# Scan runs of four fused layers: the last product by C moves to VectorE, and the second half's du is made behind the first units

## What is computed

```python
xdbl = xm @ W_xp
dtr, Bm, Cm = jnp.split(xdbl, [DTR, DTR + DS], axis=-1)
dt = jax.nn.softplus(dtr @ W_dt + b_dt)
A = -jnp.exp(A_log)

def step(hst, inp):
    dt_t, B_t, C_t, x_t = inp
    dA = jnp.exp(dt_t[:, :, None] * A)
    hst = hst * dA + (dt_t * x_t)[:, :, None] * B_t[:, None, :]
    y = jnp.einsum('bds,bs->bd', hst, C_t)
    return (hst, y)
```

## Time and profile before

| | |
|---|---|
| median of 3 runs | 1942.12 us (1942.08 to 1942.58) |
| the profiled execution | 1945.84 us, span of its instructions 1943.5 us |
| busy share of the span | PE 95%, PE weight load 69%, DVE 82%, ACT 73%, POOL 54% |
| mean granted TensorE clock | 0.975 |
| first unit of the scan, last unit (start) | 208.2 us, 1420.5 us |
| runs 0 to 5, first scan | 208.2, 446.3, 669.9, 853.7, 1083.5, 1265.7 us |

### The profile page before, as it was taken

The page is one execution under the profiler, slowest core; times in us unless marked ns, Lnnn a source line. Parts: engine busy times, 40 slices in busy tenths (PEclk is TensorE's granted clock), DMA queues, the critical chain, the costliest instruction groups (busy, mean ns, idle before and its releaser), DMA issues.

```text
span 1943.5 us, 32682 instructions
## 1 busy us (share of the span) xinstructions
PE 1845.3 (95%) x12312; PEld 1337.9 (69%) x12312; DVE 1600.7 (82%) x2125; ACT 1425.8 (73%) x2661; POOL 1048.6 (54%) x603
## 2 busy tenths in 40 slices
PE   6989899999999999999999999999998999999997
PEld 3664899948998599969995799689974333332323
DVE  5565899768998699989995999889987999999742
ACT  3426899468993899799974999799954377777775
POOL 3031599526994299939980699479944400003000
PEclk9989899998999999999999999999999799999999
DMA  5023111021111111101110121021101111111000
GB/s 202 1 85 99 59 57 55 32 72 43 56 59 37 51 54 60 51 24 55 56 44 2 40 60 56 24 72 58 58 15 32 38 42 38 37 37 36 17 23 22
DMA packets 57547, 95.18 MB, mean 49 GB/s; under 512 B 14951, under 2 KB 23559, under 8 KB 55982
## 3 DMA queue, kind: packets, MB, share of 16 engines
q1 hardware_dynamic: 55854, 88.90, 15.2%
q0 software_dynamic: 1536, 4.20, 0.7%
HBM read 73.55 MB, written 6.91 MB: 41 GB/s over the span
## 4 chain that ended last, share of the span: by engine, by line
PE 63%; POOL 14%; ACT 8%; DVE 8%; issue 6%; DMA 1%; SPq 1%; DVEq 0%; ACTq 0%; POOLq 0%
POOL A L1019 13%; PE PS L865 10%; PE PS L840 10%; PE PS L256 8%; PE PS L1603 6%; PE PS L1556 6%; PE PS L1763 5%; PE PS L846 5%; PE PS L265 3%; DVE A L1569 2%; PE PS L441 2%; PE PS L872 1%; ACT A L931 1%; ACT A L908 1%; PE PS L243 1%
## 5 line engine op out<-in xcount | busy, mean ns | idle before, releaser
L1019 POOL TENSOR_TENSOR A<-A 128x1024 f32<-128x1024 f32 x384 | 897.6, 2396 | 223.2 <-ACT small L923 111.0
L931 ACT ACTIVATE A<-A,negA 128x512 f32<-128x512 f32 x768 | 547.3, 715 | 34.0 <-DVE A L1000 24.4
L1000 DVE TENSOR_TENSOR_SCAN A<-A,PS 128x512 f32<-128x512 f32 x384 | 436.2, 1201 | 44.8 <-PE PS L846 23.8
L1000 DVE TENSOR_TENSOR_SCAN A<-A,small,PS 128x512 f32<-128x512 f32 x384 | 451.2, 1259 | 5.3 <-ACT A L931 5.3
L865 PE MATMUL PS<-ident,A 128*128 128x128 f32 x3072 | 408.5, 276 | 20.4 <-ACT A L737 13.3
L840 PE MATMUL PS<-A 128*128 128x128 f32 x3072 | 393.8, 276 | 0.9 <-ACT A L915 0.6
L865 PEld LDWEIGHTS PS<-ident,A 128*128 128x128 f32 x3072 | 352.3, 143 | 30.0 <-ACT A L737 15.9
L840 PEld LDWEIGHTS PS<-A 128*128 128x128 f32 x3072 | 368.1, 192 | 2.3 <-DVE A L1000 2.0
L1569 DVE TENSOR_REDUCE A<-PS 128x1 f32<-128x512 f32 x512 | 319.3, 681 | 38.9 <-PE PS L1556 37.3
L1800 ACT ACTIVATE A<-PS 128x512 f32<-128x512 f32 x512 | 267.2, 603 | 101.9 <-PE PS L1763 101.6
L908 ACT ACTIVATE A<-A,small 128x512 f32<-128x512 f32 x320 | 228.6, 714 | 17.3 <-PE PS L846 16.8
(11 more groups left out here) (194 smaller groups left out, 1842.7 us busy)
## 6 DMA issues: line engine op xcount, KB each, us to landing
A<-scrc SPq DMA_DIRECT2D x192, 256.0 KB, 3.1
A<-A SPq DMA_DIRECT2D x360, 32.0 KB
scr<-A SPq DMA_DIRECT2D x4, 1024.0 KB, 4.8
W<-in_wa SPq DMA_DIRECT2D x2, 1536.0 KB, 9.7
X<-in_x SPq DMA_DIRECT2D x4, 512.0 KB, 5.3
scr<-W SPq DMA_DIRECT2D x128, 1.5 KB
out<-X SPq DMA_DIRECT2D x4, 512.0 KB, 2.9
W<-in_w SPq DMA_DIRECT2D x1, 1984.0 KB, 7.3
```

The lines of the kernel that those rows point to most:

```text
L931: e.activation(A_B[i % 4], r.DT[:, dt, ci * 512:(ci + 1) * 512], ACT.Exp, scale=negA[:, r.n, dt * 16 + s:dt * 16 + s + 1]).then_inc(*decay ...
L1000: e.tensor_tensor_scan(h, a, u, init, ALU.mult, ALU.add).then_inc(*scanned.up((q, i)))
L1019: e.tensor_tensor(h, h, CB[k % 2].unsqueeze(1).broadcast_to([128, 2, 512]), ALU.mult).then_inc(*weighed.up((q, pair)))
```

## The change

- The second xd projection is copied by DVE (`copy_xd_v`), behind the relu of the first half.
- Exp, Ln, the add and the product by x work on two of the four channel blocks at a time (1024 columns). In the head only the first half's are made; the second half's Exp and Ln stand in `run_s` behind the first spreading, its add and product in `run_v` ahead of unit 4.
- All four scaled copies of the first half are made by ACT; DVE makes the plain copies of blocks 0 and 1, in all runs.
- The woven products: two in part 1 and two in part 2 (one and three before), the last four behind the first four forms of u. The product Wz Wc is split over parts 1 and 2, its bias is part 3.
- The second half's dt uses banks 4 to 7; the du transposes of both halves use banks 0 to 3; the second half's are turned at unit 4, all four in a row.
- POOL multiplies 63 pairs; DVE multiplies the last one behind its last scan. Both parts of the turning back of y come behind the last add.

```diff
-        weighed, added = sig("weighed_by_c"), sig("added_up")
+        weighed, weighed_v, added = sig("weighed_by_c"), sig("weighed_by_c_on_vector"), sig("added_up")
...
-            w.wait_ge(*act.at(("xd_twin", r.q, c)))
+            w.wait_ge(*(act if c == r.order[0] else dve).at(("xd_twin", r.q, c)))
...
-            banks.seek(3)
+            banks.seek(4)
...
-            banks.seek(4)
+            banks.seek(0)
...
-            more(3)
-            banks.seek(0)
...
+        def decline_s(e, w, r, p, d):
+            g = DUD[:, p, 2 * d:2 * d + 2, :]
+            w.wait_ge(*act.at(("abs", r.q, 2 * d + 1, r.order[p])))
+            e.activation(g, g, ACT.Exp, scale=-1.0).then_inc(*act.up(("exp", r.q, p, d)))
+        def log_s(e, w, r, p, d):
+            g = DUD[:, p, 2 * d:2 * d + 2, :]
+            w.wait_ge(*act.at(("exp", r.q, p, d)))
+            e.activation(g, g, ACT.Ln, bias=1.0).then_inc(*act.up(("ln", r.q, p, d)))
...
-            def size(p):
-                for m in range(4):
+            def size(p, d):
+                for m in range(2 * d, 2 * d + 2):
...
-            def decline(p):
-                w.wait_ge(*act.at(("abs", q, 3, r.order[p])))
-                e.activation(DUD[:, p, :, :], DUD[:, p, :, :], ACT.Exp, scale=-1.0).then_inc(*act.up(("exp", q, p)))
-            def log(p):
-                w.wait_ge(*act.at(("exp", q, p)))
-                e.activation(DUD[:, p, :, :], DUD[:, p, :, :], ACT.Ln, bias=1.0).then_inc(*act.up(("ln", q, p)))
...
-            size(0)
-            decline(0)
-            copy_xd_s(e, w, r, r.order[1])
-            log(0)
+            size(0, 0)
+            decline_s(e, w, r, 0, 0)
+            size(0, 1)
+            log_s(e, w, r, 0, 0)
+            decline_s(e, w, r, 0, 1)
+            log_s(e, w, r, 0, 1)
...
-            size(1)
+            size(1, 0)
+            size(1, 1)
...
-            decline(1)
-            log(1)
...
-            return r.G[j], Bt[:, 4 * r.order[0] + j, 0:1], r.q >= 2 and j >= 2
+            return r.G[j], Bt[:, 4 * r.order[0] + j, 0:1], j < 2
...
-        def scale_du_v(e, w, r, j):
-            g, b, _ = first_state(r, j)
-            w.wait_ge(*act.at(("bt", r.q, r.order[0])))
-            w.wait_ge(*pe.at(("dut", r.q, 0, j)))
-            e.tensor_scalar(g, bank(("dut", r.q, 0, j)), b, None, ALU.mult).then_inc(*dve.up(("scaled", r.q, j)))
+        def copy_xd_v(e, w, r, c):
+            w.wait_ge(*pe.at(("xd", r.q, c)))
+            e.tensor_copy(XD[0:96, c * 512:(c + 1) * 512], bank(("xd", r.q, c))[0:96, :]).then_inc(*dve.up(("xd", r.q, c)))
+            e.tensor_copy(XD2[64:128, c * 512:(c + 1) * 512], bank(("xd", r.q, c))[0:64, :]).then_inc(*dve.up(("xd_twin", r.q, c)))
+            banks.give(("xd", r.q, c), dve.now())
...
+            if p == 0:
+                w.wait_ge(*scaled.at((r.q, 0, j)))
...
-        def inputs_v(e, w, r, meanwhile=None, late=None):
+        def relu_v(e, w, r, p):
+            c = r.order[p]
+            for m in range(4):
+                w.wait_ge(*act.at(("abs", r.q, m, c)))
+                e.tensor_scalar(r.DT[:, m, c * 512:(c + 1) * 512], bank(("dt", r.q, m, c)), col(r.bdt, m), 0.0, ALU.add, ALU.max).then_inc(*dve.up(("relu", r.q, m, c)))
+                banks.give(("dt", r.q, m, c), dve.now())
+        def delta_v(e, w, r, p, d):
+            c = r.order[p]
+            g, t, u = DUD[:, p, 2 * d:2 * d + 2, :], r.DT[:, 2 * d:2 * d + 2, c * 512:(c + 1) * 512], r.U[:, 2 * d:2 * d + 2, c * 512:(c + 1) * 512]
+            w.wait_ge(*dve.at(("relu", r.q, 2 * d + 1, c)))
+            w.wait_ge(*act.at(("ln", r.q, p, d)))
+            e.tensor_tensor(t, t, g, ALU.add).then_inc(*dve.up(("delta", r.q, p, d)))
+            w.wait_ge(*dve.at(("delta", r.q, p, d)))
+            e.tensor_tensor(g, t, u, ALU.mult).then_inc(*dve.up(("du", r.q, p)))
+        def inputs_v(e, w, r, meanwhile=None):
...
-            for p, c in enumerate(r.order):
-                o = slice(c * 512, (c + 1) * 512)
-                for m in range(4):
-                    w.wait_ge(*act.at(("abs", q, m, c)))
-                    e.tensor_scalar(r.DT[:, m, o], bank(("dt", q, m, c)), col(r.bdt, m), 0.0, ALU.add, ALU.max).then_inc(*dve.up(("relu", q, c)))
-                    banks.give(("dt", q, m, c), dve.now())
-                if meanwhile and p == 0:
-                    meanwhile()
-                w.wait_ge(*dve.at(("relu", q, c)))
-                w.wait_ge(*act.at(("ln", q, p)))
-                e.tensor_tensor(r.DT[:, :, o], r.DT[:, :, o], DUD[:, p, :, :], ALU.add).then_inc(*dve.up(("delta", q, p)))
-                w.wait_ge(*dve.at(("delta", q, p)))
-                e.tensor_tensor(DUD[:, p, :, :], r.DT[:, :, o], r.U[:, :, o], ALU.mult).then_inc(*dve.up(("du", q, p)))
-            if late:
-                late()
-            for j in range(4):
-                if first_state(r, j)[2]:
-                    scale_du_v(e, w, r, j)
+            if meanwhile:
+                meanwhile()
+            relu_v(e, w, r, 0)
+            copy_xd_v(e, w, r, r.order[1])
+            for d in range(2):
+                delta_v(e, w, r, 0, d)
+            relu_v(e, w, r, 1)
...
-            w.wait_ge(*act.at(("xd", r.q, r.order[1])))
+            w.wait_ge(*act.at(("xd", r.q, r.order[0])))
+            w.wait_ge(*dve.at(("xd", r.q, r.order[1])))
...
-        def run_t(e, w, r, back=None, early=None):
+        def run_t(e, w, r, back=None, early=None, more=None):
...
-                        w.wait_ge(*first_copied(r, i))
+                        w.wait_ge(*act.at(("abs", q, i, r.order[1])))
+                        w.wait_ge(*dve.at(("relu", q, i, r.order[1])))
+                    if k == 1:
+                        first_half(w, r)
...
-                            w.wait_ge(*(dve.at(("scaled", q, j)) if k == 0 and first_state(r, j)[2] else scaled.at((q, k, j))))
+                            w.wait_ge(*scaled.at((q, k, j)))
...
-                w.wait_ge(*weighed.at((q, pair)))
+                w.wait_ge(*(weighed_v if pair == PAIRS_N - 1 else weighed).at((q, pair)))
...
-                if 1 <= i < 5:
-                    turn_du_t(e, w, r, 1, i - 1)
+                if i == 0 and more:
+                    banks.seek(0)
+                    more(3)
+                if i == 4:
+                    banks.seek(0)
+                    for j in range(4):
+                        turn_du_t(e, w, r, 1, j)
...
-                if pair == PAIRS_N - 1 and back:
-                    back(0)
...
+                back(0)
...
-                w.wait_ge(*dve.at(("delta", q, r.order.index(ci))))
+                w.wait_ge(*dve.at(("delta", q, r.order.index(ci), 1)))
...
-                if not first_state(r, j)[2]:
-                    scale_du_s(e, w, r, j)
+                scale_du_s(e, w, r, j)
...
+            for d in range(2):
+                decline_s(e, w, r, 1, d)
+                log_s(e, w, r, 1, d)
...
-        def run_v(e, w, r, y, back=None):
+        def run_v(e, w, r, y, back=None, late=None):
...
+                if i == 4:
+                    if late:
+                        late()
+                    for d in range(2):
+                        delta_v(e, w, r, 1, d)
...
+            w.wait_ge(*scanned.at((q, UNITS - 1)))
+            w.wait_ge(*transfer("c_load1").at((q, 31)))
+            h = r.H[(PAIRS_N - 1) % HS]
+            e.tensor_tensor(h, h, CB[1].unsqueeze(1).broadcast_to([128, 2, 512]), ALU.mult).then_inc(*weighed_v.up((q, PAIRS_N - 1)))
...
-            for pair in range(PAIRS_N):
+            for pair in range(PAIRS_N - 1):
...
-        def fuse_t(e, w, n):
+        def fuse_t(e, w, n, m):
...
-            for m in range(2):
+            if m < 2:
+                banks.seek(2 + m)
...
+                return
...
-            w.wait_ge(*pe.at(("bzc", n)))
+            w.wait_ge(*pe.at(("wzc", n, 1)))
...
-            w.wait_ge(*act.at(("wzc", 1)))
+            w.wait_ge(*pe.at(("bzc", 1)))
...
-                inputs_t(e, w, r, lambda c: w.wait_ge(*act.at(("u", b, 3))), lambda part: fuse_t(e, w, b) if part == 2 else None)
-                run_t(e, w, r, lambda p: turn_back_t(e, w, r, p, y1))
+                inputs_t(e, w, r, lambda c: w.wait_ge(*act.at(("u", b, 3))), lambda part: fuse_t(e, w, b, part - 1) if part else None)
+                run_t(e, w, r, lambda p: turn_back_t(e, w, r, p, y1), None, lambda part: fuse_t(e, w, b, part - 1))
...
-                inputs_s(e, w, r, lambda part: None)
-                run_s(e, w, r, y1, lambda part: fuse_s(e, w, b))
+                inputs_s(e, w, r, lambda part: fuse_s(e, w, b) if part == 2 else None)
+                run_s(e, w, r, y1, lambda part: None)
...
-                inputs_v(e, w, r, add_first if b else None, lambda: fuse_v(e, w, b))
+                inputs_v(e, w, r, add_first if b else None)
...
-                run_v(e, w, r, y1, lambda p: turn_back_v(e, w, r, p, YD1, ZT))
```

(11 more changed lines are left out.)

## The result

| | median us | runs | lowest to highest |
|---|---|---|---|
| before | 1942.35 | 4 | 1942.08 to 1948.18 |
| changed | 1990.06 | 4 | 1986.37 to 1992.19 |

The ratio is 1.0231, 95% interval 1.0214 to 1.0248: slower by 47.7 us, where +25 was forecast and 1975 was the upper end. The profiled execution of the changed kernel took 1992.19 us (span 1990.4, mean granted clock 0.962; before 1943.5 and 0.975). The two spans differ by 46.9 us. The direction was right. What follows looks for the 22 us that the sum lacked.

A forecast was written before the change was run, and what follows sets the result against it. ACT's full queue in the heads of the scan runs (0 to 5) was taken as the bound. Heads +17.5, C to last scan +3.4 and tail +4.1 gave +25.0: 1967.1 us, own range 1958 to 1974, 8-in-10 range 1947 to 1975.

The forecast's parts named there:

- Work of ACT in a head: ACT, each scan run's head: copies cancel, split Exp and Ln add 0.85 us a head.
- Early first scans, late C: First scans 3 to 4 us earlier, C (ACT's last du copy's end) 4 to 5 later, runs 2 to 5.
- Rival A: Heads: ACT does not bind, the early first scan carries through; 1924 us whole, 1935 by half; chance 0.10.
- The heads' sum, +17.5: Six heads, first Abs to C: -0.6, 0, +4.6, +4.9, +4.6 and +4.0 us for runs 0 to 5.
- Waits of ACT, run 2: Run 2's head: ACT waits for PE's products, 3.1 us of the +4.6 by which C comes later.
- The other heads: C later by +4.6 in run 4, +4.9 in 3, +4.0 in 5; -0.6 in run 0, 0 in 1.
- From C to the last scan: Rest of each scan run after C: PE's longer wait halves its clock, +3.4 us over six runs.
- The bound for the clock (+10): Upper bound of the stretch behind C: 145.3 us in each of the six runs, +10.0.
- The tail, +4.1: End of runs 0, 1, 3 and 5: later transposes cost +1.0 us each; nothing in runs 2 and 4.
- The steady part: Units (single DVE scans) 12 to 127: same instructions and order, no cost; up to 4.8 us a run if cover goes.
- Rival B: Heads: ACT's new waits do not come since PE reaches its products sooner; 1948 us; chance 0.17.
- Rival C: Half clock behind every C (+6.6) and DVE's products making unit 6 late (+6) add up; 1980 us; chance 0.10.

The follow-up runs named there:

- run 2: Scan run 2 of 0 to 5, inside the kernel, first of layer 2; first Abs to C 34.41 us before, 42.13 changed.
- warm: Changed kernel plus 36 identity transposes on PE ahead of each scan run's first form of u; 1973.76 us, ratio 1.0151 to before.
- run 1: Scan run 1 of 0 to 5, inside the kernel, second of layer 1; first Abs to C 36.55 us before, 39.94 changed.
- tail_alone: Kernel before with only the change's tail: last product on DVE, both turn-backs of y behind the last add; 1951.75 us, ratio 1.0033.
- run 0: Scan run 0 of 0 to 5, inside the kernel, first of layer 1; first Abs to C 37.08 us before, 41.67 changed.
- run 3: Scan run 3 of 0 to 5, inside the kernel, in layer 2; first Abs to C 35.86 us before, 42.52 changed.
- run 5: Scan run 5 of 0 to 5, inside the kernel, last of layer 2; first Abs to C 35.92 us before, 43.00 changed.
- warm_y_first: Kernel before plus 16 identity transposes ahead of pair 0's add, the change's tail, and y copied before DVE's gating; 1933.52 us, ratio 0.9936.
- run 4: Scan run 4 of 0 to 5, inside the kernel, in layer 2; first Abs to C 34.41 us before, 40.67 changed.
- xd_placed: Kernel before; DVE copies the second xd projection except in run 3, its other head work ahead of the relu in runs 1, 2; 1947.73 us, ratio 1.0013.
- tail_y_first: Kernel before with the change's tail, and DVE's copies of y ahead of its gating; 1941.09 us, ratio 0.9976.

## Why the prediction was right in direction and short in size

*Work of ACT in a head: right.* ACT's busy time in the window of run 2 rose from 34.26 to 35.42 (+1.2, where +0.85 was forecast), and a 1024-wide Exp or Ln took 1.06 as taken.

*Early first scans, late C: right.* The first scans came 3.1, 3.0, 3.3, 2.5, 3.3 and 2.8 earlier; between 2.8 and 4.1 was forecast, and each fell short by 0.3 to 0.8. Rival A fell: the fifth scan stood 4.32 for ACT's decay.

*The heads' sum, +17.5: right for the order, not for the time.* warm shows the order's cost as 17.5. The changed kernel paid 35.7. **The step that failed is the heads' sum ("Waits of ACT, run 2" and "The other heads"), which prices PE's forms and woven products at full clock.** The half clock stood in "From C to the last scan" alone. There I saw it behind C, saw that PE would stand longer, and priced that only behind C (+3.4, measured +0.6). But I had PE's next wait in my own working: the du transposes done, the scaled copies of 2.45 still to come, the forms behind them. I had moved the woven products out of that gap and then priced forms and products at full clock. The half clock fell there, ahead of the first form, and on PE's way to ACT's queue: +18.2 in the heads, of which up to 2.0 in run 1 may be DVE's wait for POOL. The bound for the clock (+10) was taken from rows behind C alone, so the range was too low. (By its own terms that range is 1959.6 to 1975.6, not 1958 to 1974; it changes nothing.) In runs 0 and 1 the bias products (L1085) stood in that slow stretch with DVE behind them, which turned forecasts of -0.6 and 0 into +4.6 and +3.4. That the move of the woven products opened the gap is read from the rows; no run put them back in the changed kernel.

The Trainium skill (TensorE: Matmul & The Clock Gate, section What's actually happening) says that an array that has been idle runs at half its clock. The trace agrees: 0.50 behind a wait of 4.18. I had cited it for the wrong place.

*The tail, +4.1: mechanism right, size short.* The gaps and the end grew by 7.5. tail_alone shows the +1.0 behind runs 0, 1 and 3. In the changed kernel the gaps behind runs 0 and 1 grew by 2.8 and 2.2, with the clock as the other part, as its PE rows show for run 0. Behind run 3 the gap shrank by 0.45, since before had a low clock there (0.73, against 1.00 now); against the 46.9 of kernels with before's tail at 1.00 it is +1.1. The 3.0 behind run 5 can't be put down to the tail, as said at tail_alone. Runs 2 to 3 and 4 to 5 did not change, as forecast (6.27).

The other rule that I weighed was one on contention. The Trainium skill (SBUF — State Buffer, section SBUF: two separate sides) lets a VectorE operation with two SBUF inputs and a GpSimd one that reads SBUF run only one at a time, each for its whole length. The trace agrees, and the wait stands inside the instruction's own length and not in a gap before it. In the tail it is small: in run 0 DVE's product began 0.17 ahead of POOL's end and took 1.25, where 1.22 is the shortest. With 0.38 us of POOL's product left it took 1.46 (run 0 of warm), and with 0.84 left 1.93 (run 0 of warm_y_first):

```profile
362.96 1.93 DVE L1007 TENSOR_TENSOR A<-A 128x1024 f32<-128x1024 f32 x1
```

Each of these ended 1.08 or 1.09 behind POOL's. The price in the changed kernel's tails is under 0.1 each, not 0.2. But I had weighed the rule for the tail alone, and it cost 2.0 in the head of run 1.

*The steady part: right in sum.* C to the last scan is 862.3 against 861.8. That is swings of the clock that cancel: run 4 is 2.8 longer, runs 3 and 0 are 1.4 and 0.9 shorter.

*Rival B fell*: the waits of ACT came. *Rival C*, half clock and DVE's products adding up, was the nearest. It named the half clock, but behind C.

What stays open: run 0's first Abs comes 3.2 us later in the profile after, in a part that was not changed. In all fourteen profiled executions this point lies between 179.9 and 187.1, in kernels alike up to there, so I take it for scatter (argued, not shown). What decides the level behind a short wait, and with it the stretch behind run 5, stays open too, and so most of what xd_placed loses. The times of one kernel spread over 6 to 9 us in xd_placed and tail_y_first.
